# Modulation made as four rows and spread by a selector, the value table waited for by key block, GpSimd clearing the whole slab

## The chip, the cores and the metric

One core of a Trainium2 chip. The metric is the device time of one execution in microseconds (us). Five engines run their own instruction streams side by side and meet only at semaphores: TensorE (PE, with its weight loads as PEld), VectorE (DVE), ScalarE (ACT), GpSimd (POOL) and SyncE (SP), which here only issues DMAs.

## The reference

The input `x` has 4 sequences of 256 tokens of width 128; `cond` has one row of 128 for each sequence.

```python
x = x + attn_ref(cond_ref(x, cond[:, None, :], ...), W_dq, W_uq, ...)   # causal, 16 heads
x = x + ffn_ref(lstm_ref(x, cond, Wx, Wh, b), w1, b1, w2, b2)

# cond_ref, hyperbolic, 16 heads, no mask
ada = t_emb @ w_ada + b_ada                       # 4 rows of 6 x 128
sh_msa, sc_msa, g_msa, sh_mlp, sc_mlp, g_mlp = split(ada, 6)
xm = expmap0(layer_norm(logmap0(x)) * (1 + sc_msa) + sh_msa)
q, k, v = (to_heads(plin(xm, w, b)) for w, b in ...)
attn_out = plin(from_heads(softmax(q k / sqrt(8)) v), w_o, b_o)
x = mobius_add(x, expmap0(g_msa * logmap0(attn_out)))
xm = expmap0(layer_norm(logmap0(x)) * (1 + sc_mlp) + sh_mlp)
ff = plin(plin(xm, w_f1, b_f1), w_f2, b_f2)
return mobius_add(x, expmap0(g_mlp * logmap0(ff)))
```

`plin(x, w, b)` is `expmap0(logmap0(x) @ w + b)`. The six parts of `ada` are one row per sequence, used for each of its 256 tokens: the first two before q, k, v, the other four after the attention. The LSTM that follows runs 256 steps in sequence, 4 sequences side by side.

## The kernel before

Each engine has one instruction stream, written out in order; an engine stands at a wait until the semaphore has its count.

The 1024 tokens are 8 tiles of 128 (tile t is sequence t % 4). Tokens are on the partitions, so a part of `ada` must lie on all 128 partitions. TensorE makes it so: ScalarE copies the transposed condition to `condT` [128, 4] and, with each column repeated 128 times, to `condR` [128, 4, 128] (lines 626 and 627); for each sequence a one-row product with `ones` brings the bias (line 1198) and a product with `condR[:, b]` as the stationary operand the rest (line 1199). That is four sequences times two column ranges (`ADA_PARTS`, line 378): columns 0 to 256 (the first two parts) into banks 1 and 2, columns 256 to 768 into banks 3 to 6, all in float32, where each product is two passes in the trace. ScalarE copies the six banks to `ada` (`ada_copies`, line 630).

The order of the front (0 to 66 us):

- VectorE: statistics of the tiles, then `front` (line 890): a first root is asked of ScalarE (`roots_in`, line 901), a ratio (line 906), a series, a second root (line 923), then `scaled` (line 896, first use of `ada`, waits for `ada_ready[0]`), `v_tm` (line 930, raises `sq_in` after each half), the norms (line 885), then q, k, v: `q_tm` (line 986) and head sums (line 982), tile by tile.
- ScalarE: clears `vaug` (line 620), `condT` and `condR`, `front_root(1)` (lines 587 to 604), two `ada_copies`, a root, four `ada_copies`, the squares of `v_tm` (line 598), two copies of the transposed tokens (line 645), a root (line 587 again), then clears the last six heads of the slab (line 648), then the squares of q, k, v tile by tile (line 652), two roots, the split of q and k (lines 658, 660).
- TensorE: a transpose of the condition (line 1192), the sixteen modulation products, eight transposes of `v_tm` (`turn8`, line 1208), q, k, v (line 1217, banks 2 to 5 in turn), then the transposes of the split q and k (line 1225).
- GpSimd: identity and mask, two casts of the identity, then clears the first `SLAB_POOL` = 10 heads of the slab (line 541) and sets a column of `vaug` (line 544).
- SP: all loads, then it waits for both slab semaphores before it fills the slab from the transposed q (line 487).

The attention of the first layer, its projection, the second half of the layer and the first rows of the causal attention follow, to 195 us. From there the LSTM steps run; TensorE, VectorE and ScalarE have fixed jobs in each step (`pe_jobs`, `vec_jobs`, `act_jobs`): the causal attention, chunk by chunk of 32 queries (`UNITS`, line 369), in the shadow of the steps. A chunk c multiplies its weights with the value table `vd` for the key blocks 0 to c (`m_values`, line 1484). Key block 0 is written by VectorE; blocks 1 to 3 and 4 to 7 come by DMA, four DMAs a block, issued by SP (line 515) behind the query fills of chunk 1 and of chunk 4. There are two semaphores, one for blocks 1 to 3 and one for 4 to 7, and TensorE waits for the whole of the first at the first unit of chunk 1 (step 11 of the LSTM) and for the whole of the second at chunk 4.

Of the kernel before, what the change touches and what calls it, by code (L numbers as in the profile page):

```python
# [24 lines left out]
ACT = mybir.ActivationFunctionType  # L25
# [5 lines left out]
B, S, D, H = 4, 256, 128, 16  # L31
HD = D // H
FF = 512
P = 128
HALVES = S // P
TILES = B * HALVES
GROUP = 4
# [35 lines left out]
CHUNKS = S // STEPS  # L73
# [2 lines left out]
ROUNDER = 1.5 * 2.0 ** 13  # L76
SMALLEST = 1e-20
W_SCALE = 16.0
SLAB_POOL = 10
SQUARES_TO_F2 = 10  # L80
A_SCALE = H_SCALE * W_SCALE
BF16_PARTS = 3
# [3 lines left out]
def adaln_attention_lstm_ffn(nc, x, cond, w_q, b_q, w_k, b_k, w_v, b_v, w_o, b_o, w_f1, b_f1, w_f2, b_f2,  # L86
                             w_ada, b_ada, W_dq, W_uq, W_dkv, W_uk, W_uv, W_o, Wx, Wh, b_g, w1, b1, w2, b2, out):
    with ExitStack() as ctx:
        def sb(name, shape, dt=F32):
            return ctx.enter_context(nc.sbuf_tensor(name, shape, dt))  # L90
# [12 lines left out]
        ones = sb("ones", [1, P])  # L103
        cond4 = sb("cond4", [B, D])
        condT = sb("condT", [P, B])
        ada_w = sb("ada_w", [P, 6 * D])
        condR = sb("condR", [P, B, P])
        ada_b = sb("ada_b", [1, 6 * D])
        ada = sb("ada", [P, B, 6, D])
        wqkv = sb("wqkv", [P, 3, D])  # L110
# [49 lines left out]
        slab_words = big[:, H * B * S // 2:].rearrange("p (h n) -> p h n", h=H)  # L160
# [7 lines left out]
        vm = vaug[:].rearrange("p t h v -> p (t h v)")[:, 0:TILES * H * (HD + 1)].rearrange("p (t h v) -> p t h v", t=TILES, h=H)  # L168
        hn = sb("hn", [P, 3, TILES, H])
        p_mla = sb("p_mla", [P, 2, 512])  # L170

        p_cond = [a[:].rearrange("p a t h d -> p a (t h d)")[:, i, :] for a in (q_sq, q_tm) for i in range(3)]
        oTs = sb("oTs", [P, 2, S])
        rd = sb("rd", [P, 2, HALVES, GROUP])
        rdm = sb("rdm", [P, H])
        mx8 = sb("mx8", [P, 2, 2 * GROUP])
# [36 lines left out]
        bank = ps("bank", [P, 8, 512])  # L213
# [13 lines left out]
        slab_zero_act = sem("slab_zero_act")  # L227
        qz_zero = sem("qz_zero")
        vd_zero = sem("vd_zero")
        v_half_mm = sem("v_half_mm")  # L230
        v_half_ready = sem("v_half_ready")
        vd_fill = [sem("vd_fill_low"), sem("vd_fill_high")]
        ones_ready = sem("ones_ready")
        dve = sem("dve_chain")
        act_ch = sem("act_chain")
        squares = sem("squares")
        cond_t = sem("cond_t")
        cond_ready = sem("cond_ready")
# [201 lines left out]
        def _(sp):  # L440
# [38 lines left out]


            sp.wait_ge(slab_zero, 1)
            sp.wait_ge(slab_zero_act, 1)
            for g in range(NG):
                sp.wait_ge(qT_ready, g + 1)
                for j in range(GROUP):
# [7 lines left out]
            for c in range(1, CHUNKS):  # L493
                if c == 1:
                    sp.wait_ge(q_half_ready, 1)
                if c == GROUP:
                    sp.wait_ge(proj_ready, PROJ.index(("q", 1, 1)) + 1)
                if c >= 2:
                    sp.wait_ge(ms_mm, units_until[c - 2])
                for h in [r * GROUP + g for g in range(NG) for r in range(GROUP)]:  # L500
                    rows = slice(h * HD, (h + 1) * HD)
                    r, g = divmod(h, GROUP)
                    sp.dma_start(qz[rows, c % 2, :, g, QB * r:QB * r + QB], q_tokens[rows, c]).then_inc(qz_fill[c % 2][g], 16)
                if c in (1, GROUP):
                    f = c // GROUP
                    if f == 0:
                        sp.wait_ge(v_half_ready, 2)
                        sp.wait_ge(vd_zero, 1)
                        sp.wait_ge(ones_ready, 1)
                    else:  # L510
                        sp.wait_ge(proj_ready, len(PROJ))
                    for kb in range(max(1, GROUP * f), GROUP * (f + 1)):
                        for r in range(GROUP):
                            keys = slice(QB * (kb % GROUP), QB * (kb % GROUP) + QB)
                            sp.dma_start(vd[QB * r:QB * r + QB, :, kb, r].rearrange("p b g v -> p b (g v)"),
                                         vm[keys, B * f:B * (f + 1), GROUP * r:GROUP * (r + 1), :].rearrange("p b h v -> p b (h v)")).then_inc(vd_fill[f], 16)
# [7 lines left out]
        def _(pool):  # L524
# [7 lines left out]
            for b in range(B):  # L532
# [2 lines left out]
                nc.gpsimd.affine_select(out=rows, in_=rows, compare_op=ALU.is_ge, fill=MASKED, base=0,  # L535
                                        pattern=[[0, 2 * GROUP], [-1, QB]], channel_multiplier=1).then_inc(consts, 1)
            pool.wait_ge(consts, 4 + B)
            nc.gpsimd.tensor_copy(identb[:], ident[:]).then_inc(consts, 1)
            nc.gpsimd.tensor_copy(identh[:], ident[:]).then_inc(consts, 1)
            for h in range(SLAB_POOL):  # L540
# [33 lines left out]
        def _(act):  # L574
# [9 lines left out]
            def root(a, y):  # L584
                taken[0] += 1
                act.wait_ge(roots_in, taken[0])
                nc.scalar.activation(y, a, ACT.Ln).then_inc(act_ch, 1)
                taken[1] += 1
                act.wait_ge(act_ch, taken[1])
                nc.scalar.activation(y, y, ACT.Exp, scale=-0.5).then_inc(roots_out, 1)  # L590
# [33 lines left out]
                nc.scalar.activation(ada_b[:, part * D:(part + 1) * D], ada_b[:, part * D:(part + 1) * D], ACT.Identity, bias=1.0).then_inc(cond_ready, 1)  # L624
            act.wait_ge(cond_t, 1)
            nc.scalar.activation(condT[:], bank[:, 0, 0:B], ACT.Copy).then_inc(cond_ready, 1)
            nc.scalar.activation(condR[:], bank[:, 0, 0:B].unsqueeze(2).to_broadcast([P, B, P]), ACT.Copy).then_inc(cond_ready, 1)
            front_root(1)

            def ada_copies(k):  # L630
                a, z = ADA_PARTS[k]
                n = z - a
                for i in range(B * n // 512):
                    act.wait_ge(ada_mm, B // 2 * k + i + 1)
                    per = 512 // n
                    nc.scalar.activation(ada[:, per * i:per * (i + 1)].rearrange("p b s d -> p b (s d)")[:, :, a:z],
                                         bank[:, 1 + 2 * k + i, :].rearrange("p (b n) -> p b n", n=n), ACT.Copy).then_inc(ada_ready[k], 1)

            ada_copies(0)
            root(col(ARG), col(ROOT))  # L640
            ada_copies(1)
            squared(v_tm)
            for k in range(2):
                act.wait_ge(v_turned, k + 1)
                nc.scalar.activation(vT[:, 4 * k:4 * k + 4, :].rearrange("p t n -> p (t n)"), bank[:, k, :], ACT.Copy).then_inc(vT_ready, 1)
            root(col(GUARDED), col(V_FACTOR))
            for h in range(SLAB_POOL, H, 2):
                ins = nc.scalar.activation(slab_words[:, h:h + 2].rearrange("p h n -> p (h n)").rearrange("p (k n) -> p k n", n=P), blank, ACT.Copy, scale=0.0)
            ins.then_inc(slab_zero_act, 1)
            for t in range(TILES):  # L650
                act.wait_ge(qkv_ready, t + 1)
                nc.scalar.activation(q_sq[:, :, t].rearrange("p a h d -> p a (h d)"),
                                     q_tm[:, :, t].rearrange("p a h d -> p a (h d)"), ACT.Square).then_inc(squares, 1)
            root(hn_x, hn[:].rearrange("p a t h -> p (a t h)"))
            root(nq[:, 1, :], nq[:, 0, :])

            act.wait_ge(qk_scaled, 1)
            nc.scalar.activation(q_pair[:, :, 0:2, :], doubled(qk_f[:, 0:TILES * H, :]), ACT.Copy).then_inc(q_high, 1)
# [529 lines left out]
        def _(pe):  # L1188
# [1 line left out]
            pe.wait_ge(consts, 4)  # L1190
            pe.wait_ge(ld_ada, 48)
            T.transpose(bank[:, 0, 0:B], cond4[:], ident[0:B, 0:B]).then_inc(cond_t, 1)
            pe.wait_ge(cond_ready, 4)
            for k, (a, z) in enumerate(ADA_PARTS):
                per = 512 // (z - a)
                for bb in range(B):
                    y = bank[:, 1 + 2 * k + bb // per, bb % per * (z - a):(bb % per + 1) * (z - a)]
                    T.matmul(y, ones[:], ada_b[:, a:z], start=True, stop=False)  # L1198
                    ins = T.matmul(y, condR[:, bb], ada_w[:, a:z], start=False, stop=True)
                    if bb % per == per - 1:  # L1200
                        ins.then_inc(ada_mm, 1)

            def turn8(src, base, signal, ready=None, count=0):
                for k in range(2):
# [8 lines left out]
            for t in range(TILES):  # L1213
                pe.wait_ge(vT_ready, 1 + t // 4)
                if t >= 4:
                    pe.wait_ge(qkv_ready, t - 3)
                T.matmul(bank[:, 2 + t % 4, 0:3 * D], vT[:, t, :], wqkv[:].rearrange("p a n -> p (a n)"), start=True, stop=True).then_inc(qkv_mm, 1)

            pe.wait_ge(consts, 10)
            for pair, low, base, signal in ((q_pair, q_low, NG, q_turned), (k_pair, k_low, 0, k_turned)):  # L1220
                pe.wait_ge(low, 1)
# [262 lines left out]
            def m_values(m):  # L1484
                c, g, bs = UNITS[m]
                pe.wait_ge(mt_ready, m + 1)
                pe.wait_ge(mo_normed, c)
                if m == FIRST_UNITS or (c == GROUP and g == 0):
                    pe.wait_ge(vd_fill[c // GROUP], 16 * GROUP * (GROUP - 1 + c // GROUP))
                for kb in range(c + 1):  # L1490
                    for j, b in enumerate(bs):
                        at = (j * (c + 1) + kb) * QB
                        n = GROUP * (HD + 1)
                        ins = T.matmul(bank[QB * b:QB * b + QB, 4, n * g:n * (g + 1)], pt_mla[:, m % 2, at:at + QB], vd[:, b, kb, :, g, :],  # L1494
                                       start=(kb == 0), stop=(kb == c), tile_position=(0, QB * b))
                ins.then_inc(mpv_mm, 1)
# [124 lines left out]
```

## Time and profile before

| what | value |
|---|---|
| runs, median (lowest to highest) | 601.0 us (600.54 to 602.06), 3 runs |
| profiled execution, its own time | 602.05 us |
| its span in the profile | 599.9 us |
| busy: PE / DVE / ACT / POOL | 452.5 / 363.9 / 302.9 / 20.0 us |
| chain that ended last: PE / DVE / ACT / issue / SP queue | 48 / 25 / 16 / 5 / 3 % |

The span is what the profiler saw of the kernel; the time of the execution is 2.15 us longer. Busy time is the sum of an engine's instructions in the span. The chain that ended last is followed back from the last instruction, at each step to what released it. L1198 is line 1198. "xN" counts records; a float32 product has two, each with one weight load.

### The profile page before, as it was taken

The page shows a single profiled execution, that of the slowest core. Times are in us where ns is not written, and L with a number is a line of the kernel's source. Part 1 is how long each engine was busy: PE and PEld are TensorE (multiplying, and loading weights), DVE is VectorE, ACT ScalarE, POOL GpSimd, SP SyncE. Part 2 cuts the span into 40 slices and gives each one's busy share as a digit, 9 for nine tenths or more (in the row PEclk, how much of TensorE's full clock was granted, in tenths as well). Part 3 has the DMA queues.
Part 4 walks back from the last instruction along what each step waited for, and adds up shares of the span by engine and source line. Part 5 has one row for each costly group of instructions (what it writes and reads, how often), then busy time and mean ns, then how long its engine had stood idle before and what let it go on. Part 6 is the DMA issues. An engine that isn't in the chain of part 4 may idle for free.

```text
span 599.9 us, 15671 instructions
## 1 busy us (share of the span) xinstructions
PE 452.5 (75%) x5551; PEld 320.1 (53%) x5551; DVE 363.9 (61%) x2041; ACT 302.9 (50%) x1356; POOL 20.0 (3%) x44
## 2 busy tenths in 40 slices
PE   4971899233937789988989999987777776866746
PEld 2231433121725678867767777675555555645544
DVE  5358333796686647777677776776545555555553
ACT  4164787352333546565555555555455445544443
POOL 5000100030200000000000000000000000000000
PEclk9995999755977655555555555575555555555555
DMA  7200300000000000010000000000000000000000
GB/s 196 73 0 1 71 2 0 2 0 1 1 1 2 14 13 7 12 20 3 4 6 2 7 3 3 2 3 3 2 6 2 6 6 2 7 6 6 2 6 5
DMA packets 17596, 7.58 MB, mean 13 GB/s; under 512 B 10245, under 2 KB 16493, under 8 KB 17518
## 3 DMA queue, kind: packets, MB, share of 16 engines
q1 hardware_dynamic: 16462, 6.06, 4.4%
q8 instruction: 44, 0.72, 0.5%
q10 hardware_dynamic: 1056, 0.52, 0.3%
q14 instruction: 34, 0.28, 0.2%
HBM read 4.02 MB, written 0.52 MB: 8 GB/s over the span
## 4 chain that ended last, share of the span: by engine, by line
PE 48%; DVE 25%; ACT 16%; issue 5%; SPq 3%; DMA 1%; ACTq 0%; DVEq 0%
PE bank L1479 8%; PE bank L1581 7%; ACT hid_a L811 5%; DVE cell L1172 5%; DVE hid L1180 4%; ACT keep L804 4%; PE bank L1254 3%; PE bank L1494 3%; PE bank L1359 3%; PE bank L1583 3%; PE bank L1242 2%; PE bank L1362 2%; PE bank L1582 2%; ACT cell_f L808 2%; PE bank L1198 2%
## 5 line engine op out<-in xcount | busy, mean ns | idle before, releaser
L1581 PE MATMUL bank<-hid,wha 128*128 128x4 f16 x1020 | 109.8, 172 | 66.4 <-DVE hid L1180 61.7
L1581 PEld LDWEIGHTS bank<-hid,wha 128*128 128x128 f16 x1020 | 89.6, 105 | 125.7 <-DVE hid L1180 124.0
L804 ACT ACTIVATE keep<-bank 128x4 f32<-128x4 f32 x256 | 44.4, 174 | 119.4 <-PE bank L1583 115.9
L1582 PE MATMUL bank<-hid,whb 128*128 128x4 f16 x1020 | 103.8, 167 | 0.0
L1583 PE MATMUL bank<-hid,whn 128*128 128x4 f16 x1020 | 103.5, 166 | 0.0
L1164 DVE SCALAR_TENSOR_TENSOR cell_a<-keep,cell 128x4 f32<-128x4 f32 x256 | 42.1, 165 | 91.8 <-ACT keep L804 89.5
L1582 PEld LDWEIGHTS bank<-hid,whb 128*128 128x128 f16 x1020 | 91.7, 107 | 1.9 <-issue 0.2
L1479 PE MATMUL bank<-kT,big 128*128 128x64 f32 (+6 forms) x224 | 92.1, 536 | 0.0
L811 ACT ACTIVATE hid_a<-cell 128x8 f32<-128x8 f32 x256 | 54.3, 212 | 73.4 <-DVE cell L1172 73.4
L1583 PEld LDWEIGHTS bank<-hid,whn 128*128 128x128 f16 x1020 | 87.6, 103 | 0.0
L1180 DVE TENSOR_TENSOR_SCAN hid<-hid_f,hid_a 128x20 f16<-128x20 f32 x256 | 50.9, 199 | 52.6 <-ACT hid_a L811 52.4
L1479 PEld LDWEIGHTS bank<-kT,big 128*128 128x128 f32 x224 | 53.8, 313 | 0.0
L1172 DVE TENSOR_TENSOR_SCAN cell<-cell_f,cell_a 128x16 f32<-128x16 f32 x256 | 49.0, 191 | 4.7 <-ACT cell_f L808 0.3
L808 ACT ACTIVATE cell_f<-bank 128x8 f32<-128x8 f32 x256 | 47.0, 184 | 0.3 <-PE bank L1362 0.3
L806 ACT ACTIVATE emit<-bank 128x4 f32<-128x4 f32 x256 | 44.3, 173 | 0.0
L1167 DVE TENSOR_SCALAR hid_f<-emit 128x8 f32<-128x8 f32 x256 | 43.4, 170 | 0.0
L1176 DVE RECIPROCAL hid_f<-hid_f 128x4 f32<-128x4 f32 x256 | 40.3, 157 | 0.4 <-issue 0.4
L743 ACT ACTIVATE p_mla<-bank,mx 128x64 f32<-128x64 f32 (+6 forms) x112 | 39.9, 378 | 0.0
L1494 PE MATMUL bank<-big,q_sq 128*32 128x36 f32 x1120 | 38.3, 254 | 2.1 <-DMA big<-vaug 2.1
L1182 DVE TENSOR_TENSOR v_tm<-hid_f,hid_a 128x4 f32<-128x4 f32 x256 | 35.3, 138 | 0.1
L1494 PEld LDWEIGHTS bank<-big,q_sq 128*32 128x32 f32 x1120 | 31.9, 157 | 2.8 <-DVE q_sq L1114 2.2
L1102 DVE TENSOR_REDUCE mx<-bank 128x2 f32<-128x320 f32 (+6 forms) x44 | 25.5, 578 | 1.3
(274 smaller groups left out, 722.1 us busy)
## 6 DMA issues: line engine op xcount, KB each, us to landing
big<-qT SPq DMA_DIRECT2D x112, 4.0 KB
big<-big SPq DMA_DIRECT2D x16, 64.0 KB, 2.0
x_tm<-in_x ACTq DMA_DIRECT2D x2, 256.0 KB, 3.8
wf<-in_L_cond_w_f SPq DMA_DIRECT2D x2, 256.0 KB, 5.3
x_tb<-in_x SPq DMA_DIRECT2D x4, 128.0 KB, 3.0
big<-vaug SPq DMA_DIRECT2D x28, 18.0 KB, 1.9
out_y<-tb SPq DMA_DIRECT2D x7, 64.0 KB, 1.9
ada_w<-in_L_cond_w_ada SPq DMA_DIRECT2D x1, 384.0 KB
```

The costliest lines, as they stand in the source:

```text
L804: nc.scalar.activation(keep[:, k, :], keep_bank(c)[:, i], ACT.Tanh, scale=1.0 / A_SCALE).then_inc(keep_act, 1)
L806: nc.scalar.activation(emit[:, k, :], emit_bank(c)[:, i], ACT.Tanh, scale=1.0 / A_SCALE).then_inc(emit_act, 1)
L808: nc.scalar.activation(cell_f[:, k, :, 1:3].rearrange("p b s -> p s b"), new_bank(c)[:, i], ACT.Tanh, scale=1.0 / A_SCALE).then_inc(new_ac ...
L811: nc.scalar.activation(hid_a[:, k, :, 0:4:3], cell[:, k, :, 3].unsqueeze(2).to_broadcast([P, B, 2]), ACT.Tanh, scale=-1.0).then_inc(th_act, 1)
L1167: V.tensor_scalar(hid_f[:, k, :, 1:5:3], emit[:, k, :].unsqueeze(2).to_broadcast([P, B, 2]), 1.0, SMALLEST, ALU.add, ALU.max).then_inc(sig ...
L1172: V.tensor_tensor_scan(cell[:, k].rearrange("p b s -> p (b s)"), cell_f[:, k].rearrange("p b s -> p (b s)"), cell_a[:, k].rearrange("p b s ...
L1180: V.tensor_tensor_scan(hid[:, k].rearrange("p b s -> p (b s)"), hid_f[:, k].rearrange("p b s -> p (b s)"), hid_a[:, k].rearrange("p b s -> ...
L1479: ins = T.matmul(bank[:, m % 2, j * keys:(j + 1) * keys], qz[:, c % 2, bs[j], g, :], kT_tokens[:, bs[j], 0:keys], start=False, stop=True, ...
L1494: ins = T.matmul(bank[QB * b:QB * b + QB, 4, n * g:n * (g + 1)], pt_mla[:, m % 2, at:at + QB], vd[:, b, kb, :, g, :], start=(kb == 0), sto ...
L1581: T.matmul(acc, wha[:, gate, :], hid[:, k, :, 2], start=False, stop=True, skip_group_check=True)
L1582: T.matmul(acc, whb[:, gate, :], hid[:, k, :, 2], start=False, stop=True, skip_group_check=True)
L1583: ins = T.matmul(acc, whn[:, gate, :], hid[:, k, :, 4], start=False, stop=True, skip_group_check=True)
```

## The change

- `condR` and its copy go. TensorE makes four rows (one per sequence, on partitions 0 to 3) of the 768 columns: for columns 0 to 256 and then 256 to 768 a bias product and a product with `condT` as the stationary operand. ScalarE copies them to `ada_rows`, both copies ahead of `front_root(1)`.
- GpSimd writes a selector `batch_of` [4, 4, 128], row b of which is one for sequence b. TensorE spreads the rows by products with `batch_of[:, b]`: the first two parts for all four sequences, then the four later parts for sequences 0 and 1; those for sequences 2 and 3 come behind q, k, v. ScalarE's copies follow the same order.
- GpSimd clears all 16 heads of the slab; ScalarE's clears and their semaphore go.
- The value table has a semaphore for each key block, and TensorE waits at the first unit of each chunk c for block c alone.

```diff
-SLAB_POOL = 10
+SLAB_POOL = H
-        condR = sb("condR", [P, B, P])
+        ada_rows = p_mla[0:B].rearrange("p a n -> p (a n)")[:, 0:6 * D]
+        batch_of = oTs[0:B].rearrange("p a n -> p (a n)").rearrange("p (b n) -> p b n", b=B)
-        vd_fill = [sem("vd_fill_low"), sem("vd_fill_high")]
+        vd_fill = [sem(f"vd_fill{kb}") for kb in range(CHUNKS)]
+        REST_BANK = (6, 7, 0, 1)
 # SP
             sp.wait_ge(slab_zero, 1)
-            sp.wait_ge(slab_zero_act, 1)
...
-                             vm[keys, ...]).then_inc(vd_fill[f], 16)
+                             vm[keys, ...]).then_inc(vd_fill[kb], 16)
 # GpSimd
             pool.wait_ge(consts, 4 + B)
+            nc.gpsimd.tensor_copy(batch_of, ident[0:B, 0:B].unsqueeze(2).to_broadcast([B, B, P])).then_inc(batch_ready, 1)
             nc.gpsimd.tensor_copy(identb[:], ident[:]).then_inc(consts, 1)
 # ScalarE
-            nc.scalar.activation(condR[:], bank[:, 0, 0:B].unsqueeze(2).to_broadcast([P, B, P]), ACT.Copy).then_inc(cond_ready, 1)
+            for k, (a, z) in enumerate(ADA_PARTS):
+                act.wait_ge(ada_rows_mm, k + 1)
+                nc.scalar.activation(ada_rows[:, a:z], bank[0:B, 5 + k, 0:z - a], ACT.Copy).then_inc(ada_rows_ready, 1)
             front_root(1)
-            ada_copies(0)
+            for i in range(2):
+                ada_low(i)          # waits ada_mm >= i + 1, banks 1 + i, two sequences each
             root(col(ARG), col(ROOT))
-            ada_copies(1)
+            for b in range(2):
+                ada_rest(b)         # waits ada_mm >= 3 + b, bank REST_BANK[b]
             squared(v_tm)
...
             root(col(GUARDED), col(V_FACTOR))
-            for h in range(SLAB_POOL, H, 2):
-                ins = nc.scalar.activation(slab_words[:, h:h + 2]..., blank, ACT.Copy, scale=0.0)
-            ins.then_inc(slab_zero_act, 1)
...
             root(nq[:, 1, :], nq[:, 0, :])
+            for b in range(2, B):
+                ada_rest(b)
 # TensorE
-            pe.wait_ge(cond_ready, 4)
+            pe.wait_ge(cond_ready, 3)
             for k, (a, z) in enumerate(ADA_PARTS):
-                per = 512 // (z - a)
-                for bb in range(B):
-                    y = bank[:, 1 + 2 * k + bb // per, bb % per * (z - a):(bb % per + 1) * (z - a)]
-                    T.matmul(y, ones[:], ada_b[:, a:z], start=True, stop=False)
-                    ins = T.matmul(y, condR[:, bb], ada_w[:, a:z], start=False, stop=True)
-                    if bb % per == per - 1:
-                        ins.then_inc(ada_mm, 1)
+                T.matmul(bank[0:B, 5 + k, 0:z - a], ones[:, 0:B], ada_b[:, a:z], start=True, stop=False)
+                T.matmul(bank[0:B, 5 + k, 0:z - a], condT[:], ada_w[:, a:z], start=False, stop=True).then_inc(ada_rows_mm, 1)
+            pe.wait_ge(batch_ready, 1)
+            def ada_rest(b):
+                T.matmul(bank[:, REST_BANK[b], :], batch_of[:, b, :], ada_rows[:, 2 * D:6 * D], start=True, stop=True).then_inc(ada_mm, 1)
+            pe.wait_ge(ada_rows_ready, 1)
+            for b in range(B):
+                ins = T.matmul(bank[:, 1 + b // 2, b % 2 * 2 * D:(b % 2 + 1) * 2 * D], batch_of[:, b, :], ada_rows[:, 0:2 * D], start=True, stop=True)
+                if b % 2:
+                    ins.then_inc(ada_mm, 1)
+            pe.wait_ge(ada_rows_ready, 2)
+            for b in range(2):
+                ada_rest(b)
...
 # turn8 of v_tm, then q, k, v
+            for b in range(2, B):
+                ada_rest(b)
+            pe.wait_ge(ada_ready[1], 4)
             pe.wait_ge(consts, 10)
...
 # in m_values
-                if m == FIRST_UNITS or (c == GROUP and g == 0):
-                    pe.wait_ge(vd_fill[c // GROUP], 16 * GROUP * (GROUP - 1 + c // GROUP))
+                if g == 0 and bs[0] == 0:
+                    pe.wait_ge(vd_fill[c], 16 * GROUP)
```

## Rows read from the trace of the kernel before

**Rows 1.** Chain of waits, first 66 us: start us, us, what.

```profile
31.21 2.02 PE bank L1199 x2
...
36.37 2.84 ACT big L648 x3
```

**Rows 2.** Timeline of PE, first 66 us: start us, us, engine, line, out<-in, xcount, [idle before].

```profile
7.92 1.22 PE L1198 MATMUL bank<-ada_b,ones 1*128 1x256 f32 x2 [2.62 <-ACT condR L627]
9.07 1.22 PE L1199 MATMUL bank<-ada_w,condR 128*128 128x256 f32 x2
...
17.12 2.07 PE L1198 MATMUL bank<-ada_b,ones 1*128 1x512 f32 x2
19.12 2.08 PE L1199 MATMUL bank<-ada_w,condR 128*128 128x512 f32 x2
...
33.01 1.79 PE L1208 MATMUL bank<-ident,v_tm 128*128 128x128 f32 x8
35.52 4.11 PE L1217 MATMUL bank<-wqkv,vT 128*128 128x384 f32 x12 [0.72 <-ACT vT L645]
...
57.99 5.56 PE L1225 MATMUL bank<-identh,big 128*128 128x128 f16 x64 [15.25 <-DVE big L1014]
```

**Rows 3.** Timeline of ACT, first 66 us.

```profile
7.24 0.15 ACT L626 ACTIVATE condT<-bank 128x4 f32<-128x4 f32 x1
...
9.74 0.21 ACT L587 ACTIVATE small<-small 128x8 f32<-128x8 f32 x1 [1.88 <-DVE small L901]
...
33.75 1.14 ACT L598 ACTIVATE tb<-v_tm 128x512 f32<-128x512 f32 x2
34.78 1.07 ACT L645 ACTIVATE vT<-bank 128x512 f32<-128x512 f32 x2
35.92 0.21 ACT L587 ACTIVATE small<-small 128x8 f32<-128x8 f32 x1
```

**Rows 4.** Timeline of DVE, first 66 us.

```profile
8.51 1.20 DVE L901 TENSOR_SCALAR small<-small 128x8 f32<-128x8 f32 x1
...
14.18 0.17 DVE L923 TENSOR_SCALAR small<-small 128x8 f32<-128x8 f32 x1
17.94 2.19 DVE L896 SCALAR_TENSOR_TENSOR ta<-x_tm,mv,ada 128x128 f32<-128x128 f32 x8 [3.59 <-ACT ada L636]
...
20.84 2.19 DVE L930 SCALAR_TENSOR_TENSOR v_tm<-ta,small,ada 128x128 f32<-128x128 f32 x8
...
37.28 1.14 DVE L986 SCALAR_TENSOR_TENSOR q_tm<-bank,small,bqkv 128x384 f32<-128x384 f32 x2
39.65 0.55 DVE L982 TENSOR_REDUCE hn<-q_sq 128x48 f32<-128x384 f32 x1 [1.23 <-ACT q_sq L652]
...
45.57 1.22 DVE L982 TENSOR_REDUCE hn<-q_sq 128x48 f32<-128x384 f32 x2
```

**Rows 5.** Timeline of POOL, first 66 us.

```profile
4.71 4.72 POOL L541 MEMSET big<- 128x512 f32 x10
9.37 0.31 POOL L544 MEMSET vaug<- 128x128 f32 x1
```

**Rows 6.** Groups of POOL by line: busy us, mean ns, idle before.

```profile
L559 POOL CAST p_mla<-bg 1x512 bf16<-1x512 f32 x3 | 1.8, 599 | 21.5 <-ACT bg L694 21.4
```

**Rows 7.** Timeline of all engines, 144 to 152 us.

```profile
147.02 3.74 PE L1322 MATMUL bank<-wf,vT 128*128 128x512 f32 x4 [0.69 <-ACT vT L710]
```

**Rows 8.** Stretches of PE: us, busy (count), granted clock, DMA share, GB/s.

```profile
8.00:10.00 2.00, 2.00 (x4) 1.00 0.79 229
...
147.00:148.00 1.00, 0.98 (x1) 0.50 0.00 0
150.00:151.00 1.00, 1.00 (x5) 0.70 0.00 0
```

**Rows 9.** Timeline of PE, 186 to 220 us.

```profile
213.79 0.47 PE L1494 MATMUL bank<-big,q_sq 128*32 128x36 f32 x16 [2.09 <-DMA big<-vaug]
```

**Rows 10.** Timeline of the SP queue, 186 to 240 us.

```profile
203.43 8.99 SPq L515 DMA_DIRECT2D big<-vaug  x12
```

More of the change, by code:

```diff
@@ L226, in adaln_attention_lstm_ffn @@
         slab_zero = sem("slab_zero")
-        slab_zero_act = sem("slab_zero_act")
         qz_zero = sem("qz_zero")
@@ L238, in adaln_attention_lstm_ffn @@
         cond_ready = sem("cond_ready")
+        ada_rows_mm = sem("ada_rows_mm")
+        ada_rows_ready = sem("ada_rows_ready")
+        batch_ready = sem("batch_ready")
         ada_mm = sem("ada_mm")
@@ L515, in _ @@
                             sp.dma_start(vd[QB * r:QB * r + QB, :, kb, r].rearrange("p b g v -> p b (g v)"),
-                                         vm[keys, B * f:B * (f + 1), GROUP * r:GROUP * (r + 1), :].rearrange("p b h v -> p b (h v)")).then_inc(vd_fill[f], 16)
+                                         vm[keys, B * f:B * (f + 1), GROUP * r:GROUP * (r + 1), :].rearrange("p b h v -> p b (h v)")).then_inc(vd_fill[kb], 16)
             for p, (c, a, z) in enumerate(PIECES):
@@ L626, in _, with ada_low @@
             nc.scalar.activation(condT[:], bank[:, 0, 0:B], ACT.Copy).then_inc(cond_ready, 1)
-            nc.scalar.activation(condR[:], bank[:, 0, 0:B].unsqueeze(2).to_broadcast([P, B, P]), ACT.Copy).then_inc(cond_ready, 1)
+            for k, (a, z) in enumerate(ADA_PARTS):
+                act.wait_ge(ada_rows_mm, k + 1)
+                nc.scalar.activation(ada_rows[:, a:z], bank[0:B, 5 + k, 0:z - a], ACT.Copy).then_inc(ada_rows_ready, 1)
             front_root(1)
[L630 to L637, printed above, removed]
-            ada_copies(0)
+            def ada_low(i):
+                act.wait_ge(ada_mm, i + 1)
+                nc.scalar.activation(ada[:, 2 * i:2 * i + 2, 0:2, :], bank[:, 1 + i, :].rearrange("p (b s d) -> p b s d", b=2, d=D), ACT.Copy).then_inc(ada_ready[0], 1)
+            def ada_rest(b):
+                act.wait_ge(ada_mm, 2 + b + 1)
+                nc.scalar.activation(ada[:, b, 2:6, :], bank[:, REST_BANK[b], :].rearrange("p (s d) -> p s d", d=D), ACT.Copy).then_inc(ada_ready[1], 1)
+            for i in range(2):
+                ada_low(i)
             root(col(ARG), col(ROOT))
-            ada_copies(1)
+            for b in range(2):
+                ada_rest(b)
             squared(v_tm)
@@ L646, in _ @@
             root(col(GUARDED), col(V_FACTOR))
-            for h in range(SLAB_POOL, H, 2):
-                ins = nc.scalar.activation(slab_words[:, h:h + 2].rearrange("p h n -> p (h n)").rearrange("p (k n) -> p k n", n=P), blank, ACT.Copy, scale=0.0)
-            ins.then_inc(slab_zero_act, 1)
             for t in range(TILES):
@@ L1192, in _, with ada_rest @@
             T.transpose(bank[:, 0, 0:B], cond4[:], ident[0:B, 0:B]).then_inc(cond_t, 1)
-            pe.wait_ge(cond_ready, 4)
+            pe.wait_ge(cond_ready, 3)
             for k, (a, z) in enumerate(ADA_PARTS):
-                per = 512 // (z - a)
-                for bb in range(B):
-                    y = bank[:, 1 + 2 * k + bb // per, bb % per * (z - a):(bb % per + 1) * (z - a)]
-                    T.matmul(y, ones[:], ada_b[:, a:z], start=True, stop=False)
-                    ins = T.matmul(y, condR[:, bb], ada_w[:, a:z], start=False, stop=True)
-                    if bb % per == per - 1:
-                        ins.then_inc(ada_mm, 1)
+                T.matmul(bank[0:B, 5 + k, 0:z - a], ones[:, 0:B], ada_b[:, a:z], start=True, stop=False)
+                T.matmul(bank[0:B, 5 + k, 0:z - a], condT[:], ada_w[:, a:z], start=False, stop=True).then_inc(ada_rows_mm, 1)
+            pe.wait_ge(batch_ready, 1)
+            def ada_rest(b):
+                T.matmul(bank[:, REST_BANK[b], :], batch_of[:, b, :], ada_rows[:, 2 * D:6 * D], start=True, stop=True).then_inc(ada_mm, 1)
[7 more added lines that the diff above has]
+                ada_rest(b)
             def turn8(src, base, signal, ready=None, count=0):
```

## The prediction

> **What bounds the kernel now.** I read the chain of waits first, in order of time. From 7.9 to 33.2 us it is nothing but TensorE: the products of lines 1198 and 1199, one pair after the other [rows 1]. So the modulation is the chain for 25 us, and every engine behind it waits. The timeline of TensorE shows why it is long: a one-row bias product of 256 columns starts at 7.92 and the next product at 9.07 (1.15 us each), the 512-column ones are 2.00 us apart, and there are eight of each kind [rows 2]: 8 x 1.15 + 8 x 2.00 = 25.2 us. VectorE had the normalised tokens ready long before: its last `v_tm` instruction row begins at 20.84 and lasts 2.19, so it is through at 23.03 [rows 4], while their transposes start only at 33.01 [rows 2]. Then the chain runs through ScalarE, where three slab-clearing instructions stand 2.84 us in it [rows 1]. From 195 us the 256 LSTM steps follow one another; there the only wait on a transfer is 2.09 us for the value table [rows 9].
>
> **Part 1, four rows and a selector.** TensorE starts when ScalarE has written `condT`: 7.24 + 0.15 = 7.39 [rows 3], instead of waiting for `condR` until 7.92. The rows are two products of 256 columns and two of 512, at the old starts-apart 2 x 1.15 + 2 x 2.00 = 6.3 us [rows 2], so they end at 7.43 + 6.3 = 13.73. No row has a stationary operand of four columns; I take the full duration and let the bounds be half of it and the whole of it (half is the gap between the two clock levels, below).
>
> ScalarE takes its instructions in order, and both row copies now stand ahead of `front_root(1)`. Its logarithm ran at 9.74 [rows 3]. The second copy starts at 13.75 and takes about 0.53, half of the two 512-wide copies of 1.07 [rows 3]; the logarithm starts at 14.3. From it to the end of VectorE's line 923 was 14.35 - 9.74 = 4.61 us [rows 3, 4], which gives 18.9. Meanwhile the first spread, four products of 1.15, ends at 18.35, and its second copy at 18.95. So `scaled` starts at 18.97 where it started at 17.94 [rows 4]: this part first loses 1.0 us. From there to the end of `v_tm` is 23.03 - 17.94 = 5.09, hence 24.06, with the first half (four of eight instructions of 0.27) at 22.96.
>
> TensorE spends 2 x 2.00 on two of the four later parts, until 22.35, and is free when the first half of `v_tm` comes. Eight transposes took 1.79 [rows 2], so the second four end near 24.06 + 0.9 + 0.2 = 25.15. ScalarE squares for 0.57 a half [rows 3], until 24.65, then copies twice 0.53 (the second copy from 25.2), and reaches the logarithm of `V_FACTOR` at 25.8; it was at 35.92 [rows 3]. Gain to here 10.1 us. The other two later parts come behind q, k, v: two products on TensorE and two copies (1.2 us) on ScalarE. They cost nothing: TensorE stood 15.25 us between q, k, v and the turns of the split q [rows 2], and the two copies stand in the same stretch, behind ScalarE's roots, while VectorE still scales q and k. Without that cover each product would cost 2.0 and each copy 0.6.
>
> **Part 2, the slab on GpSimd.** ScalarE's 2.84 us go [rows 1]. What they held up is less: after two `q_tm` instructions (37.28 + 1.14 = 38.42) VectorE waited for the first square until 39.65 [rows 4], 1.23 us. Now the logarithm at 25.8 puts `q_tm` at 25.8 + 1.36 = 27.16, two of them end at 28.3, and the sum of squares follows at once. 39.65 - 28.3 = 11.35 us in all. The rest of that loop runs to 45.57 + 1.22 = 46.79 [rows 4] at VectorE's pace as before.
>
> GpSimd's own stream grows. Ten clears in 4.72 are 0.47 each, and the stream ended at 9.37 + 0.31 = 9.68 [rows 5]. Six more are 2.8, and the selector copy, 512 elements wide, I put at 0.6 by the 512-wide cast [rows 6]: end near 13.1. That matters, because VectorE's small `TENSOR_SCALAR` of line 901 took 1.20 us from 8.51, until 9.71, while the same operation of line 923 took 0.17 [rows 4]: it stood until GpSimd's stream was over. It will now stand until 13.1. ScalarE is not there before 14.3, so the cover is 1.2 us. The Trainium skill, SBUF — State Buffer, section Who interferes with whom, has the pair of ports held as an exclusive lock for a whole instruction. By that rule VectorE would get in between two clears, near 9; the row shows otherwise, and in the sum both are hidden.
>
> **Part 3, the clock.** Over 8 to 10 us the granted clock reads 1.00 [rows 8], but a 512-column pass pair took 2.0 us there, while at 147.02 two such products took 3.74 [rows 7] with 0.50 in the column [rows 8]. So the modulation ran at the 1.2 GHz level. By 35.52 q, k, v ran at 4.11 / 6 = 0.685 us a tile [rows 2], the 2.4 GHz level; ahead of the rise TensorE had done the last `ada_w` products and eight transposes. At 147.02 it rose after 3.6 us of work, in the stretch 150 to 151 [rows 8]. In the new order the transposes begin at 23 and q, k, v at 25.1, so I take the rise at about 28: the first two tiles cost 1.37 (twice 0.685), the second is ready at 28.1, and its `q_tm` starts 0.5 late (27.6 planned). Bounds: 0, and 2.8 us where all eight tiles are slow: the last would be ready at 26.8 + 7 x 1.37 = 36.4, against 33.6. I take 0.5. The Trainium skill, TensorE: Matmul & The Clock Gate, in its closing advice for kernels, says that a TensorE kept busy without gaps comes to full rate after about 4 us. By that rule the modulation would have left 1.2 GHz near 12 us; the rows say it did not. Were it right for the new order, the rival "fast rows" below would come true.
>
> **Part 4, the value table.** Twelve transfers are issued over 8.99 us from 203.43 [rows 10]; TensorE got on at 213.79, after 2.09 us [rows 9]. The first key block needs the first four: issued by about 206.5. The last of the twelve was issued by 212.42 and TensorE went on 1.4 us later, so the fourth is there by 208, with 2 us to spare even at twice that, before TensorE comes at 213.79 - 2.09 = 211.7. The wait goes whole, -2.09. Its successor in the chain is TensorE's own work of that step (0.47 plus a projection of 1.2), as before. Blocks 2 and 3 are landed by 214, and are wanted 12 and 24 steps later. The five new waits behind find their semaphores raised. SP's order is untouched.
>
> **Sum.** -11.35 + 0.5 - 2.09 = -12.9 us. The profiled execution took 602.05, so 589.1; the median of the runs is 601.0, 1.05 lower, so **588.1 us**.
>
> **Rivals.**
> *Fast rows* (the 2.4 GHz level from the rows on). For: those products have no gap. Against: neither had the old ones. Rows would end near 10.6, then GpSimd's 13.1 sets the logarithm (1.2 earlier), transposes are quicker by some 0.4 and the 0.5 of part 3 goes: 588.1 - 2.1 = 586.0. Chance 0.12.
> *q, k, v slow to the end*: 2.8 instead of 0.5, 590.4. For: selector products use four rows only and one-row products stood in the slow stretch. Against: from 23 on the work is like that before the old rise. Chance 0.13.
> *The value wait is replaced* by another at the same step: 590.2. For: TensorE has little slack there. Against: it was idle the whole 2.09 for this one releaser. Chance 0.06.
> *GpSimd holds VectorE, slower than before.* One mechanism: line 901 stands until the stream ends, and the stream now has the selector copy, an operation no row shows. It decides from 14.3 us on, and the kernel gets slower once the copy costs over 14 us more. At 33 ns an element, 17 us, the stream ends at 29.6, 15.3 after 14.3: 603.4. Against: 512 elements cost 0.6 in the cast [rows 6]. Chance 0.02.
> A smaller slip of the same sort (copies, first spread, GpSimd by 1 to 2 us) lies inside the range, 0.07.
>
> **How the numbers follow.** The forecast itself has 0.60. Its own spread is 587 to 589.3. The range reaches to the fast rows below and to the slow tiles above: 585.8 to 590.8. Within 0.3% is about what can be told from no change. Only the GpSimd case is not faster, so 0.97 faster, 0.01 the same, 0.02 slower.
>
> **What would show it.** Rows: line 1198's successor ends near 13.7; the logarithm near 14.3, line 901 ending near 13.1; `v_tm` ends near 24.1; `hn` of the last tile near 36; no `DMA big<-vaug` wait at the twelfth step; LSTM steps begin 10.8 us earlier. Wrong if the logarithm runs past 15, if q, k, v tiles stay over 1.3 us, or if the span after 195 us shrinks by other than 2.1.

## The result and the profile after

The changed kernel takes 587.83 us (median of 4 runs, 587.35 to 589.03); the kernel before, on the same chips, 601.53. The ratio is 0.9767, with a 95% interval of 0.9747 to 0.9786: 13.7 us less. Forecast were 588.1 us and 12.9 less. The profiled execution took 589.03 us; two lines of its page:

```profile
span 586.9 us, 15661 instructions
...
PE 441.3 (75%) x5543; PEld 315.8 (54%) x5543; DVE 367.7 (63%) x2041; ACT 301.0 (51%) x1354; POOL 23.4 (4%) x51
```

The span is 13.0 us shorter. The timeline of TensorE in the first 60 us, columns as in [rows 2]:

```profile
7.43 1.01 PE L1201 MATMUL bank<-ada_b,ones 1*4 1x256 f32 x2 [1.94 <-ACT condT L630]
8.37 1.01 PE L1202 MATMUL bank<-ada_w,condT 128*4 128x256 f32 x2
9.32 1.86 PE L1201 MATMUL bank<-ada_b,ones 1*4 1x512 f32 x2
11.11 1.87 PE L1202 MATMUL bank<-ada_w,condT 128*4 128x512 f32 x2
12.91 3.78 PE L1210 MATMUL bank<-p_mla,oTs 4*128 4x256 f32 x8
16.48 3.62 PE L1206 MATMUL bank<-p_mla,oTs 4*128 4x512 f32 x4
22.23 2.17 PE L1222 MATMUL bank<-ident,v_tm 128*128 128x128 f32 x8 [2.13 <-DVE v_tm L936]
24.52 6.96 PE L1231 MATMUL bank<-wqkv,vT 128*128 128x384 f32 x16
31.41 1.98 PE L1206 MATMUL bank<-p_mla,oTs 4*128 4x512 f32 x4
46.32 6.22 PE L1242 MATMUL bank<-identh,big 128*128 128x128 f16 x64 [12.93 <-DVE big L1020]
```

Four products with a stationary operand of four columns (lines 1201 and 1202) and six spreads (1210 and 1206) have taken the place of sixteen. From 7.43 to 20.1 TensorE is busy without a gap, then it waits 2.13 us for `v_tm`: VectorE is now what it waits for. ScalarE and VectorE, the rows that answer to [rows 3] and [rows 4]:

```profile
13.02 0.59 ACT L633 ACTIVATE p_mla<-bank 4x512 f32<-4x512 f32 x1 [3.22 <-PE bank L1202]
13.51 0.19 ACT L591 ACTIVATE small<-small 128x8 f32<-128x8 f32 x1
...
23.26 0.63 ACT L602 ACTIVATE tb<-v_tm 128x512 f32<-128x512 f32 x1 [0.42 <-DVE v_tm L936]
...
24.93 0.20 ACT L591 ACTIVATE small<-small 128x8 f32<-128x8 f32 x1
```

```profile
8.45 4.37 DVE L907 TENSOR_SCALAR small<-small 128x8 f32<-128x8 f32 x1
...
17.93 0.17 DVE L929 TENSOR_SCALAR small<-small 128x8 f32<-128x8 f32 x1
18.14 2.19 DVE L902 SCALAR_TENSOR_TENSOR ta<-x_tm,mv,ada 128x128 f32<-128x128 f32 x8
...
21.04 2.19 DVE L936 SCALAR_TENSOR_TENSOR v_tm<-ta,small,ada 128x128 f32<-128x128 f32 x8
...
26.29 0.62 DVE L992 SCALAR_TENSOR_TENSOR q_tm<-bank,small,bqkv 128x384 f32<-128x384 f32 x1
27.46 0.62 DVE L992 SCALAR_TENSOR_TENSOR q_tm<-bank,small,bqkv 128x384 f32<-128x384 f32 x1 [0.55 <-PE bank L1231]
...
33.90 1.22 DVE L988 TENSOR_REDUCE hn<-q_sq 128x48 f32<-128x384 f32 x2
```

And GpSimd, answering to [rows 5] (the selector copy and the clears):

```profile
4.25 0.60 POOL L541 COPY oTs<-ident 4x512 f32<-4x512 f32 x1
...
5.27 7.51 POOL L545 MEMSET big<- 128x512 f32 x16
```

Marks along the way, by the start of an instruction or, for the sums, its end:

| mark | before | after | less |
|---|---|---|---|
| logarithm of the first root (ScalarE) | 9.74 | 13.51 | -3.8 |
| `scaled` (VectorE) | 17.94 | 18.14 | -0.2 |
| logarithm for `V_FACTOR` (ScalarE) | 35.92 | 24.93 | 11.0 |
| last head sum ends (VectorE) | 46.79 | 35.12 | 11.67 |
| first turn of the split q (TensorE) | 57.99 | 46.32 | 11.67 |
| first score product (TensorE) | 64.46 | 53.48 | 10.98 |
| first product of the second half, line 1322 before | 147.02 | 136.06 | 10.96 |
| LSTM step 0 (`keep`, ScalarE) | 194.79 | 184.25 | 10.54 |
| LSTM step 12 | 215.84 | 203.15 | 12.69 |
| LSTM step 40 | 262.04 | 248.78 | 13.26 |
| end of the span | 599.9 | 586.9 | 13.0 |

Three things happen: the front wins 11.67, some 1.1 of it is lost again before the LSTM, and the loop adds 2.2 at the value table and 0.5 around step 30, of which 0.3 go again behind step 40.

### The profile page after: what moved, and what is told of

Same layout as the page of the kernel before. It is cut to its first block, busy times and chain, and to the rows that moved or that the text cites. A ratio compares the mean times of both kernels' runs of the same rounds, so it can differ in the third digit from the quotient of the medians.

```text
span 586.9 us, 15661 instructions
## 1 busy us (share of the span) xinstructions
PE 441.3 (75%) x5543; PEld 315.8 (54%) x5543; DVE 367.7 (63%) x2041; ACT 301.0 (51%) x1354; POOL 23.4 (4%) x51
## 4 chain that ended last, share of the span: by engine, by line
PE 48%; DVE 30%; ACT 15%; issue 6%; SPq 0%; DMA 0%; POOL 0%; DVEq 0%; POOLq 0%
PE bank L1496 9%; PE bank L1598 7%; ACT hid_a L817 5%; DVE cell L1178 5%; DVE hid L1186 5%; ACT keep L810 4%; PE bank L1271 3%; PE bank L1511 3%; DVE cell_a L1170 3%; PE bank L1376 3%; PE bank L1600 3%; PE bank L1259 3%; PE bank L1599 2%; PE bank L1379 2%; DVE mx L1108 2%
## 5 line engine op out<-in xcount | busy, mean ns | idle before, releaser
L1496 PE MATMUL bank<-kT,big 128*128 128x64 f32 (+6 forms) x224 | 89.7, 524 | 0.0
L1496 PEld LDWEIGHTS bank<-kT,big 128*128 128x128 f32 x224 | 52.2, 303 | 0.0
```

What stands on the lines that cost most here:

```text
L1496: ins = T.matmul(bank[:, m % 2, j * keys:(j + 1) * keys], qz[:, c % 2, bs[j], g, :], kT_tokens[:, bs[j], 0:keys], start=False, stop=True, ...
```

## The experiments

The kernel before was timed again beside each group of runs: 601.53 us beside the changed kernel, 602.31 beside x1 to x4, 603.13 beside x5 to x8, 602.98 beside x9 and x10. So runs of different groups are set against each other by their ratio to it, or by their spans, and not by their times.

**1. The value table alone.** The changed kernel with the old wait, and the kernel before with the new one:

```diff
 # x1_old_value_wait, from the changed kernel (and two semaphores in place of eight)
-                if g == 0 and bs[0] == 0:
-                    pe.wait_ge(vd_fill[c], 16 * GROUP)
+                if m == FIRST_UNITS or (c == GROUP and g == 0):
+                    pe.wait_ge(vd_fill[c // GROUP], 16 * GROUP * (GROUP - 1 + c // GROUP))
 # x2_only_value_wait: the reverse edit, and nothing else, in the kernel before
```

> The changed kernel with the value table waited for as before (all of blocks 1 to 3 at chunk 1, all of 4 to 7 at chunk 4). My theory: the wait is a price of its own, 2.1 us at step 11 and nothing elsewhere; against the kernel before the gain shrinks from 13.7 to about 11.6, near 589.9 us, and TensorE shows one wait of 2.1 us for the vaug transfers. Rival, the LSTM steps swallow it (the step 11 work is late anyway): the gain stays at 13.7. Rival, the front alone made 13.7: same.

> The kernel before with the value table waited for by key block and nothing else. My theory: 2.1 us less, about 599.4, all of it between steps 11 and 12; the front to the us as before. Rival: the wait is replaced by one on the transposed weights or on TensorE's own work, under 0.5 us.

Measured: x1 591.17 us, ratio to before 0.9814 (0.9789 to 0.9839), against 0.9767 with the new wait; x2 599.72 us, ratio 0.9963 (0.9947 to 0.9979), that is 2.2 us. TensorE's first value product in the changed kernel, in x1 and in x2:

```profile
201.11 0.47 PE L1511 MATMUL bank<-big,q_sq 128*32 128x36 f32 x16
```

```profile
203.21 0.47 PE L1511 MATMUL bank<-big,q_sq 128*32 128x36 f32 x16 [1.61 <-DMA big<-vaug]
```

```profile
211.60 0.47 PE L1494 MATMUL bank<-big,q_sq 128*32 128x36 f32 x16
```

Only x1 shows a wait. From step 11 to step 12 the kernel before takes 4.34 us, x1 3.86, the changed kernel 2.18 and x2 2.17. x1's span is 2.4 us longer than the changed kernel's, 1.7 of it here and 0.5 in steps 30 to 40, which experiment 5 comes to. The wait is a price of its own, worth 1.7 to 2.2 us, and nothing took its place. x2's front stands to the hundredth where it stood (last head sum 46.79).

**2. ScalarE's clears.**

```diff
 # x3_scalar_clears, from the changed kernel
-SLAB_POOL = H
+SLAB_POOL = 10
+            for h in range(SLAB_POOL, H, 2):     # ScalarE, behind the root of V_FACTOR
+                ins = nc.scalar.activation(slab_words[:, h:h + 2]..., blank, ACT.Copy, scale=0.0)
+            ins.then_inc(slab_zero_act, 1)
 # SP waits for this semaphore too, as before
```

> The changed kernel with ScalarE clearing the last six heads of the slab again. My theory from the trace of the changed kernel: ScalarE is through its root at 25.4, the clears end at 28.2, the first square at 28.7, the first head sum starts there and not at 27.99: 0.7 us more, since q, k, v are late now too and cover part of it. VectorE's stalled root request ends near 10 and not at 12.8, which changes nothing, as ScalarE comes only at 13.5. Rival: the whole 2.8 us come back. Rival: the shorter GpSimd stream matters more, and it gets faster by up to 0.7.

Measured: 588.99 us, ratio 0.978 (0.9755 to 0.9805), an interval that overlaps the changed kernel's. The trace settles it; its last row of head sums is

```profile
34.58 1.22 DVE L993 TENSOR_REDUCE hn<-q_sq 128x48 f32<-128x384 f32 x2
```

It ends at 35.80 instead of 35.12, 0.7 later. The clears on ScalarE were worth 0.7 us and not 2.84: VectorE has its first two `q_tm` to do meanwhile (in the kernel before it waited 1.23 us for the first square [rows 4]), and here the slow q, k, v products hold up the second of them by 0.55, which covers another part.

**3. The stalled root request.** Line 901 of the kernel before (907 after) took 1.20 us in the kernel before [rows 4] and 4.37 in the changed one, where another `TENSOR_SCALAR` of its size takes 0.17. First the clears were moved away from it, then gaps were put between them:

```diff
 # x4_clears_later, from the changed kernel (GpSimd)
+            pool.wait_ge(qkv_ready, 1)
             for h in range(SLAB_POOL):
 # x10_gaps_in_clears, from the changed kernel (GpSimd)
-                ins = nc.gpsimd.memset(slab_words[:, h, :], 0.0)
-            ins.then_inc(slab_zero, 1)
+                nc.gpsimd.memset(slab_words[:, h, :], 0.0).then_inc(slab_zero, 1)
+                pool.wait_ge(slab_zero, h + 1)
 # SP then waits for all 16
```

> The changed kernel with GpSimd's clears held back until the first q, k, v tile is written. My theory: the 4.4 us of VectorE's root request in the changed kernel are GpSimd's clears; it now takes 0.2 and ends near 8.6. The time does not change (within 0.3 us), since ScalarE's logarithm waits for the second row copy at 13.5 anyway. Rival: the 4.4 us are a wait of another kind (ScalarE or a transfer) and stay. Rival: the stall set the pace of the front, and 0.7 us or more are won.

> The changed kernel with a wait of GpSimd on its own semaphore after each of the 16 clears, which leaves a gap between them. It measures the stall by itself. Theory A: VectorE's request is let in as soon as GpSimd has no clear queued behind the running one: it ends by about 9.1 instead of 12.82. Theory B: it stands as long as the stream has clears, gap or not: about 13.5. The time of the whole doesn't change in either (ScalarE comes at 13.5), within 0.5 us.

Measured: x4 587.9 us, ratio 0.9764 (0.9743 to 0.9785), the time of the changed kernel. VectorE's request in x4:

```profile
8.84 0.17 DVE L908 TENSOR_SCALAR small<-small 128x8 f32<-128x8 f32 x1
```

In x10, with the clears running beside it (VectorE, then GpSimd):

```profile
8.61 0.17 DVE L907 TENSOR_SCALAR small<-small 128x8 f32<-128x8 f32 x1
```

```profile
5.27 9.24 POOL L545 MEMSET big<- 128x512 f32 x16
```

With gaps the request passes in 0.17 us in the middle of 9.2 us of clears; behind clears without gaps it stands to their end. (In x10 it came 0.1 us before a gap, so this run doesn't tell what it pays behind a clear that has just begun.) Theory A holds, and the stall is GpSimd's doing. In neither run does `scaled` move (18.15 and 18.14), so in the changed kernel the stall is hidden, as forecast. x10's single time of 591.59 us was expected to stay within 0.5 of the changed kernel. It did not (its span is 2.4 us longer), and not because of the stall: its last head sum is 0.3 late, its LSTM step 0 is 0.84 late and it loses 1.5 more in two places of the loop that experiment 5 comes to.

**4. The row work in the order of need.** In the changed kernel the second row copy stands ahead of the first root on ScalarE, and TensorE makes all rows before it spreads the first.

The edit, its orders written in words:

```diff
 # x6_rows_in_turn, from the changed kernel and x4
 # ScalarE
-            copies of both row parts; front_root(1)
+            root; copy of row part 0; the two logarithms of front_root(1)
             ada_low(0), ada_low(1); root
-            ada_rest(0), ada_rest(1)
+            copy of row part 1
...
-            for b in range(2, B): ada_rest(b)      # behind the roots of q, k, v
+            for b in range(B): ada_rest(b)
 # TensorE
-            rows 0, rows 1, first spread, rest 0 and 1, turns, q, k, v, rest 2 and 3
+            rows 0, first spread, rows 1, turns, q, k, v, rest 0 to 3
 # x9_in_turn_early_clears: x6 without the added pool.wait_ge(qkv_ready, 1)
```

> The changed kernel with the row work in the order of need: the root first on ScalarE, then the copy of the first row part; TensorE spreads the first two parts before it makes the rows of the later four; all four later spreads behind q, k, v; GpSimd's clears held back as in the run above. My theory: scaled starts near 14.1 instead of 18.14, the transposes near 18.2, and the head sums end near 31.0 instead of 35.1: 4 us less, near 583.8 us. Rival: the TensorE clock costs part back (q, k, v at the slow level longer, later rises), 2 us less. Rival: the later spreads behind q, k, v now hold up the split of q and k: nothing.

> The reordered kernel with GpSimd's clears where the change has them, from 5.3 us on. Here ScalarE is free early, so VectorE's root request is on the path. My theory: it stands until the clears are over, 12.8, the root follows there, scaled starts near 17.5 instead of 14.45, and 3.0 us of the reordered kernel's 3.3 are lost: between 588 and 588.5 us, about that of the change. Rival, by the rule that the ports are held for one instruction: the request gets in between two clears, under 0.5 us lost.

Measured: x6 585.7 us, ratio 0.9713 (0.9696 to 0.973), clear of the changed kernel's interval: about 3 us faster than it, and the fastest of all. x9 588.57 us, ratio 0.9763 (0.9746 to 0.978). TensorE in x6:

```profile
9.95 3.75 PE L1219 MATMUL bank<-p_mla,oTs 4*128 4x256 f32 x8 [0.56 <-ACT p_mla L635]
13.63 1.86 PE L1208 MATMUL bank<-ada_b,ones 1*4 1x512 f32 x2
15.42 1.87 PE L1209 MATMUL bank<-ada_w,condT 128*4 128x512 f32 x2
18.55 2.17 PE L1229 MATMUL bank<-ident,v_tm 128*128 128x128 f32 x8 [1.26 <-DVE v_tm L942]
20.84 7.02 PE L1238 MATMUL bank<-wqkv,vT 128*128 128x384 f32 x16
27.79 4.12 PE L1215 MATMUL bank<-p_mla,oTs 4*128 4x512 f32 x8
```

```profile
14.45 2.19 DVE L908 SCALAR_TENSOR_TENSOR ta<-x_tm,mv,ada 128x128 f32<-128x128 f32 x8 [0.74 <-ACT ada L645]
```

`scaled` starts at 14.45 instead of 18.14 and the last head sum ends at 31.44, 3.7 us earlier than in the changed kernel; 31.0 was expected, and 583.8 us for the whole. LSTM step 0 comes 3.5 earlier. The four later spreads behind q, k, v hold up nothing. In x9 the request is on the path:

```profile
8.47 4.34 DVE L912 TENSOR_SCALAR small<-small 128x8 f32<-128x8 f32 x1
...
18.20 2.19 DVE L907 SCALAR_TENSOR_TENSOR ta<-x_tm,mv,ada 128x128 f32<-128x128 f32 x8 [0.74 <-ACT ada L644]
```

It ends at 12.81; the root follows at 12.85 and, since the copy of the first rows now stands behind the root on ScalarE, the first spread too: `scaled` starts at 18.20, and all 3.7 us are gone. So a stall that costs nothing in the changed kernel costs about 3 us here, and the order that wins needs both edits.

**5. TensorE's clock.** Why did 25 us of unbroken products run at the slow duration?

```diff
 # x5_no_bias_products, from the kernel before: the bias of the modulation is left out
-                    T.matmul(y, ones[:], ada_b[:, a:z], start=True, stop=False)
-                    ins = T.matmul(y, condR[:, bb], ada_w[:, a:z], start=False, stop=True)
+                    ins = T.matmul(y, condR[:, bb], ada_w[:, a:z], start=True, stop=True)
 # x7_full_selector, from the changed kernel: selector and rows on 128 partitions, zeros below the four
+            V.memset(batch_all, 0.0); V.memset(ada_all, 0.0)     # VectorE, before x comes
-            ... batch_of[:, b, :], ada_rows[:, a:z] ...
+            ... batch_all[:, b, :], ada_all[:, a:z] ...
 # GpSimd and ScalarE wait for the two clears
 # x8_in_turn_full: x6 with the same edit
```

> The kernel before without the eight one-row bias products (the bias of the modulation is left out of the result). It tells why the modulation ran at the slow duration for 25 us. Theory A: the one-row products between kept TensorE at 1.2 GHz; without them the 128-row products rise to the 2.4 GHz level some 4 us after they begin at 7.9 (512 columns in 0.86 instead of 2.0), and the modulation is over near 16 to 17. Theory B: the slow level has to do with the time since the start or with the loads still running until 22 us; then 8 products at the slow pace, 4 x 0.9 + 4 x 1.8 = 10.6, end near 18.5. In both the front gains more than the share of the products.

> The changed kernel with selector and rows 128 partitions deep (zeros below the four), cleared by VectorE while it waits for x. The products are the same in columns. Theory A (thin operands keep TensorE at the slow level): the spread starting at 12.9 rises to the fast level some 4 us later, q, k, v run fast from the first tile, and 0.5 to 1.0 us are won. Theory B (it rises by time or busy share, whatever the rows): no difference, within 0.2 us in the front.

> Both of the last two edits. Theory A: another 0.5 to 1.5 us below the reordered one, as its q, k, v come when TensorE is already fast. Theory B: equal to the reordered one.

Measured: x5 589.16 us (one run). Its eight products, TensorE's timeline and one of its weight loads:

```profile
7.90 6.87 PE L1198 MATMUL bank<-ada_w,condR 128*128 128x256 f32 x16 [2.45 <-ACT condR L627]
18.50 2.17 PE L1207 MATMUL bank<-ident,v_tm 128*128 128x128 f32 x8 [3.73 <-DVE v_tm L930]
```

```profile
12.03 0.19 PEld L1198 LDWEIGHTS bank<-ada_w,condR 128*128 128x128 f32 x1 [0.24 <-issue]
```

They take 6.87 us, where sixteen took 25.3: from 11.2 on one 512-column pass comes every 0.43 us, where a 256-column pass took as long before, and a weight load takes 0.19 instead of 0.33. In the kernel before, with a one-row product between any two, the pace stayed slow to the end. The rule of the Trainium skill, TensorE: Matmul & The Clock Gate, section Why this matters for your kernels (about 4 us of unbroken work), fits x5 and not the kernel before. The granted clock reads 1.00 in every run up to the first stretch that is recorded at the 1.2 GHz level (from 34.5 us on in the changed kernel, from 17.7 in x5), also where the durations are those of that level already; up to there only the durations tell the level. x7, with the same number of columns as the changed kernel:

```profile
12.91 3.13 PE L1217 MATMUL bank<-p_mla,oTs 128*128 128x256 f32 x8
15.88 1.88 PE L1213 MATMUL bank<-p_mla,oTs 128*128 128x512 f32 x4
22.24 2.16 PE L1229 MATMUL bank<-ident,v_tm 128*128 128x128 f32 x8 [4.48 <-DVE v_tm L943]
24.53 7.56 PE L1238 MATMUL bank<-wqkv,vT 128*128 128x384 f32 x16
```

```profile
22.00:24.00 2.00, 1.76 (x8) 0.52 0.00 0
24.00:28.00 4.00, 3.88 (x8) 0.50 0.00 0
28.00:30.00 2.00, 2.00 (x7) 0.78 0.00 0
```

Its 512-column spreads end after 1.88 us, where the changed kernel's took 3.62: theory A of the level is right, on 128 rows it rises at about 15.3. But the time is 591.69 us, ratio 0.981 (0.9794 to 0.9827), slower than the changed kernel, where 0.5 to 1.0 us were expected to be won. The early rise won nothing: TensorE is through early and waits 4.48 us for `v_tm`, the level falls at 22.1, and q, k, v start slow again, until 28.9 (0.50 in the rows above; 27.7 in the changed kernel), and take 7.56 us instead of 6.96. That the gap made the kernel slower is not shown, though: in x10, which has the thin operands, q, k, v take 7.56 us as well. In x7 this costs 0.3 us at the last head sum (35.42), which is made up by the first product of the second half (135.93 against 136.06). Of the 1.6 us by which its span is longer, the larger part comes later: 1.0 between the first product of the second half and step 0 (185.12), as in x10 (185.09), and 0.34 each in steps 0 to 10 and 40 to 50, where x8 loses the same against x6 and no run without the wide operands does. Why was not tested.

x8 is 586.79 us, ratio 0.9731 (0.971 to 0.9752), no faster than x6 either, where theory A gave it 0.5 to 1.5 us. The idle time ahead of its turns is 2.95 us. Its q, k, v take 6.70 us instead of 7.02 and its step 0 comes 0.7 earlier than x6's, but its span is only 0.3 shorter: the loop takes the rest back.

The clock accounts for the 1.1 us lost behind the front as well. TensorE's granted clock around the turns of the split q (stretch, length, busy, count, granted clock), before and after:

```profile
61.00:62.00 1.00, 1.00 (x14) 0.57 0.28 66
...
241.00:251.00 10.00, 9.31 (x147) 0.50 0.05 8
```

```profile
46.00:51.00 5.00, 4.68 (x45) 0.50 0.12 28
51.00:52.00 1.00, 1.00 (x16) 0.72 0.11 23
...
228.00:238.00 10.00, 8.50 (x161) 0.78 0.05 8
```

Before, the level rose at 61.9, 3.9 us after the first turn; after, at 51.6, 5.2 us after it. So the 64 turns take 6.22 us instead of 5.56 [rows 2], and 0.7 are gone. At the products of the second half it rose 3.6 us after the first one before and 4.3 after, and another 0.4 is lost by step 0. These moments differ from run to run: from the last head sum to step 0 it is 148.0 us in the two runs with the old front (before and x2), and 148.5 to 149.7 in the ten with an earlier one, so an earlier front loses 0.5 to 1.7 us here. In the loop the clock gives: the kernel before has 0.50 from 241 to 251, the changed one rises once at the corresponding steps (0.78 from 228 to 238), and steps 30 to 40 take 15.29 us instead of 15.81. Over all runs these ten steps take 15.3 (after, x2, x4, x6, x7, x8, x9) or 15.8 (before, x1, x3, x5, x10); in each of the seven the level is up for a stretch there, in none of the five. Steps 120 to 130, the same instructions each time, take 15.8 to 17.1 us: 17.11 in x6 and 17.10 in x10, 16.15 in the changed kernel. That is where x10's 1.5 us went (0.5 and 1.0), and most of the 1.3 by which x6's span, 2.2 us shorter than the changed kernel's, falls behind its gain of 3.5 at step 0; by the ratios of the timed runs x6 gains about 3. What decides in which steps the clock rises was not tested by itself.

## Why the prediction was right

- *The chain and what replaces it*: right. TensorE's 25 us were the chain, and VectorE's chain to `v_tm` took over; forecast `v_tm` ready at 24.06, measured 23.23.
- *Rows and spread at the old durations*: too dear by 0.8 us. The row products came at 0.95 and 1.8, not 1.15 and 2.00, and the spreads at 0.89 and 1.8, so the logarithm ran at 13.51, not 14.3, and the loss at `scaled` was 0.2 us and not 1.0. This term alone makes the front 11.67 instead of 10.85.
- *ScalarE's clears*: the forecast took 1.2 us for them before the slow products; x3 shows 0.7 of them on top of the slow products, which overlap them. The sum of both, 1.2 less 0.5, is what was measured.
- *GpSimd's stream and VectorE's request*: forecast end 13.1, measured 12.82; hidden, as x4 shows. It ended with the last of the sixteen clears (12.78) and not, as the forecast read the old rows, with the stream (13.05). The sentence on the port rule is borne out half: the row's reading (it stands to the end of the clears) is right for clears without gaps, and x10 shows that one gap lets it in, so the rule of the Trainium skill, SBUF — State Buffer, Who interferes with whom (an exclusive lock for a whole instruction), fits x10 and not the kernels before and after.
- *Slow first tiles of q, k, v*: forecast 0.5 late, measured: the second `q_tm` waited 0.55 us for its product.
- *The clock afterwards*: missed. The forecast left everything behind the front as it was. Some 1.1 us were lost before the LSTM and 0.5 won at step 30. One of its own signs failed by this: the span after 195 us (from step 0 on) was to shrink by 2.1 and shrank by 2.5, from 405.1 to 402.6.
- *Value table*: forecast 2.09, measured 2.16, and by x1 and x2 1.7 to 2.2.

So 588.1 against 587.8 is in part luck: 0.8 us that the sum gave the rows too much stand against about 0.6 net of clock effects that were not in the sum. The gain itself was 13.7 us and not 12.9; the two times agree more closely because the kernel before came out 0.5 above the 601.0 that the forecast started from. The rivals: the fast rows did not come, nor did q, k, v stay slow; no new wait took the place of the value wait; GpSimd's copy cost 0.60 us, to the hundredth that of the cast.

## What to carry to other kernels

Broadcasting a few rows by a selector costs as many columns as making them broadcast, but the expensive operand and its bias are then run through once; what it gains is read from what the next engine waits for, and it is worth ordering the rows, the spreads and the copies by who is late. Zeroing work belongs where its engine is idle and its neighbour sends nothing short: before it is moved to GpSimd, look for short `TENSOR_SCALAR` instructions of VectorE beside it. Waits between the clears let such an instruction in (x10), at 9.24 us for the clears instead of 7.51. Split a wait by what its first reader needs; that was 2 us for one line.

## What the runs showed of the hardware

- A VectorE `TENSOR_SCALAR` of 8 columns stood 4.37 us behind GpSimd clears without gaps, 0.17 us beside the same clears with a wait between them; `SCALAR_TENSOR_TENSOR` of the same size kept its 0.17 beside them (lines 904 and 905).
- A float32 pass with a stationary operand of 4 columns came 0.10 us sooner than with 128 (0.47 against 0.575 for 256 columns), in a series where the two kinds of product alternate.
- TensorE, busy without a gap from 7.9 to 33 us with a one-row product at every other place, kept the durations of the 1.2 GHz level; without these products it had those of the 2.4 GHz level after 3.3 us. Once the level is up, thin products are fast too: in x8 a 512-column product with one row takes 1.02 us, in x6 1.86.
- The granted clock reads 1.00 up to the first stretch recorded at the 1.2 GHz level and is not to be trusted there: in the changed kernel the durations up to 27.7 us are those of the 1.2 GHz level.
